# A gather ring that also borrows the buffers of rows needed later, and products spread evenly over a tile

## The reference, cut to what matters

```
xn  = layernorm(x)
xp  = xn @ W                                   # 4 heads of 256
e   = leaky_relu(a_src[src] + a_dst[dst])      # per edge and head, also a loop per node
alpha = softmax of e over the edges of a destination
x1  = x + relu(segment_sum(xp[src] * alpha, dst) + bias)
out = x1 + quantize(layernorm(x1)) @ quantize(weight).T + ffn_bias
```

## Time and profile before

| | |
|---|---|
| median of 3 runs | 1280.57 us |
| the profiled execution's own time | 1283.93 us |
| its span | 1282.0 us |
| busy: PE, PEld, DVE, ACT, POOL | 79%, 45%, 75%, 51%, 55% of the span |
| gathers (queue 0) | 211.80 MB |
| mean granted clock of TensorE | 0.898 of full |
| last stage | about 482 to 1282 us |

### The profile page before, as it was taken

One profiled execution on the slowest core, in us unless ns is written; L12 is line 12 of the kernel. 1 busy time (PEld: TensorE's weight loads), 2 busy tenths in 40 slices (PEclk: granted clock), 3 DMA queues, 4 the chain that ended last, 5 costly groups with the idle time before them and its releaser, 6 DMA issues.

```text
span 1282.0 us, 32738 instructions
## 1 busy us (share of the span) xinstructions
PE 1009.4 (79%) x12460; PEld 574.0 (45%) x12485; DVE 961.6 (75%) x2213; ACT 654.6 (51%) x887; POOL 711.3 (55%) x668
## 2 busy tenths in 40 slices
PE   8799488899999985556767777888888778877764
PEld 6678244455445532333433444444444444444332
DVE  6998899988986346666676778888878888778650
ACT  4566488788446534233342554544554544455541
POOL 1000367666214735765667777777777777777100
PEclk9899699999999996557887999898999999989888
DMA  7686358655347538888999999999999999999310
GB/s 276 204 302 242 80 177 305 208 175 167 99 148 222 168 119 294 294 271 268 328 317 331 329 375 379 363 359 363 381 366 358 354 356 358 366 342 354 136 40 23
DMA packets 126624, 339.75 MB, mean 265 GB/s; under 512 B 33135, under 2 KB 46719, under 8 KB 126218
## 3 DMA queue, kind: packets, MB, share of 16 engines
q0 software_dynamic: 75104, 211.80, 46.6%
q1 hardware_dynamic: 48010, 125.00, 28.0%
q10 hardware_dynamic: 3360, 0.91, 0.4%
HBM read 331.32 MB, written 56.04 MB: 302 GB/s over the span
## 4 chain that ended last, share of the span: by engine, by line
DMA 21%; PE 17%; issue 9%; POOL 6%; DVE 5%; ACT 3%; DVEq 1%; POOLq 0%; ACTq 0%
DMA xg<-d_xp,tables 14%; PE fmm_ps L2115 9%; PE sum_ps L2087 6%; DMA acc<-d_xp,tables 4%; POOL xg L1824 4%; POOL acc L1824 2%; DMA acc<-d_xp,first_idx 2%; PE ftr_ps L2099 2%; DVE acc L1864 1%; ACT own_row L2011 1%; DMA xg<-d_xp,first_idx 1%; PE fmm_ps L2112 0%; DVE acc L1931 0%; DVE fscale L1922 0%; ACT q L2028 0%
## 5 line engine op out<-in xcount | busy, mean ns | idle before, releaser
L1824 POOL DMA_INDIRECT xg<-d_xp,tables x292 | 312.9, 1072 | 120.8 <-issue 70.0
L2011 ACT ACTIVATE own_row<-acc,ratio 32x256 f32<-32x256 f32 x392 | 197.9, 505 | 244.1 <-DVE acc L1889 231.7
L2115 PE MATMUL fmm_ps<-wdT,xqT 128*128 128x512 f16 x1200 | 312.8, 407 | 0.0
L1864 DVE TENSOR_TENSOR acc<-sum_ps,acc 128x258 f32 x488 | 205.9, 422 | 115.9 <-PE sum_ps L2090 104.8
L1605 PE MATMUL xp_ps<-acc 128*128 128x512 f16 x1152 | 262.9, 381 | 7.4 <-DVE acc L1163 4.7
L2087 PE MATMUL sum_ps<-xg,tables 128*32 128x256 f16 x3564 | 169.8, 308 | 118.8 <-DMA xg<-d_xp,tables 43.6
L1824 POOL DMA_INDIRECT acc<-d_xp,tables x186 | 199.4, 1072 | 62.4 <-issue 42.4
L2115 PEld LDWEIGHTS fmm_ps<-wdT,xqT 128*128 128x128 f16 x1200 | 115.9, 104 | 146.1 <-issue 40.5
L1605 PEld LDWEIGHTS xp_ps<-acc 128*128 128x128 f16 x1152 | 109.1, 98 | 128.5 <-DVE acc L1163 4.5
L2087 PEld LDWEIGHTS sum_ps<-xg,tables 128*32 128x32 f16 x3564 | 75.4, 102 | 203.4 <-issue 94.2
L2087 PE MATMUL sum_ps<-acc,tables 128*32 128x256 f16 x2292 | 96.6, 281 | 49.6 <-DMA acc<-d_xp,tables 34.4
(11 more groups left out here) (353 smaller groups left out, 1632.7 us busy)
## 6 DMA issues: line engine op xcount, KB each, us to landing
d_xnT<-acc SPq DMA_DIRECT2D x25, 512.0 KB, 3.7
own_row<-d_own SPq DMA_DIRECT2D x25, 512.0 KB
wdT<-in_x_dram SPq DMA_DIRECT2D x24, 512.0 KB, 5.0
acc<-d_xnT SPq DMA_DIRECT2D x24, 512.0 KB, 4.9
d_xp<-acc SPq DMA_DIRECT2D x24, 512.0 KB
d_own<-acc SPq DMA_DIRECT2D x96, 128.0 KB
tables<-d_lo SPq DMA_DIRECT2D x33, 320.0 KB, 4.9
xr<-in_x_dram SPq DMA_DIRECT2D x16, 512.0 KB, 7.2
```

The lines of the kernel that those rows point to most:

```text
L1824: nc.gpsimd.indirect_dma_start(out=xg[j].rearrange("p a n -> p (a n)"), out_offset=None, in_=d_xp, in_offset=bass.IndirectOffsetOnAxis(ap= ...
L1864: nc.vector.tensor_tensor(out=to, in0=sum_ps[k % SB][:, 0:AW], in1=to, op=ALU.add).then_inc(added, 1)
L2011: last = nc.scalar.activation(own_row[r % 2][q * WIN:(q + 1) * WIN, h * C:(h + 1) * C], sums[rows, r * TILE_WINS + q, 0:C], ACT.Relu, scal ...
L2115: last = nc.tensor.matmul(mm_ps[:, cols], xqT[:, a, c, :], wdT[:, c, b, cols], start=False, stop=(c == KC - 1 and a == 1), skip_group_chec ...
```

## The change

- `ring_of_slots`: four more buffers take gathers from slot 0 on, each until a given slot: the buffer of normalised rows `xn` (until 28), `xr[0]` (20), `xr[1]` (38) and `own_row[0]` (9). Slots 0 to 8 so have nine buffers, then fewer, and from 41 to 53 five as before. The five spare places join at slot READY[j] + 14 (54, 75, 95, 115, 136), before at READY[j] + 40 (80, 101, 121, 141, 162), and their first gather waits for `moved` of the tile (the end of `move(j, 1)`) where it waited for the transposition.
- Normalised rows have one buffer of their own, `xn`, so the spare places hold them no more; `norm(r)` also waits for the transposition of tile r-1. Small scratch tiles lie in the end of `tables`, which was unused.
- The first loads of `own_row[0]`, `xr[0]` and `xr[1]` wait for the last gather slot in them (8, 15 and 35), the load of `own_row[1]` goes ahead of those of x, and the third load of x waits for `moved` of tile 0.
- `CHUNK` is 5 where it was 7: 10 bundles (9 of 5, one of 3) behind every second slot, 20 of 20.3 slots.

```
+EARLY = {"xn": 28, "xr0": 20, "xr1": 38, "own0": 9}
+FIRST_SPARE = RING + len(EARLY)
...
-    free_from = [(0, j) for j in range(RING)] + [(READY[j] + TURN_AT + 8, RING + n) for n, j in enumerate(SPARE_TILES)]
+    free = [(0, SLOTS_ALL, j) for j in range(RING)] + [(0, until, RING + n) for n, until in enumerate(EARLY.values())]
+    free += [(READY[j] + 14, SLOTS_ALL, FIRST_SPARE + n) for n, j in enumerate(SPARE_TILES)]
...
-    CHUNK = 7
+    CHUNK = 5
...
+        xn = sb("xn", [P, D])[:, :]
+        xg += [a.bitcast(F16).rearrange("p (a n) -> p a n", a=2)
+               for a in [xn, xr[0], xr[1], own_row[0][:, :]] + [of_tile(j) for j in SPARE_TILES]]
...
             def load_own(r):
+                if r == 0:
+                    sp.wait_ge(slot_done, EARLY_LAST["own0"] + 1)
...
             def load_x(r):
+                if r < 2:
+                    sp.wait_ge(slot_done, EARLY_LAST[f"xr{r}"] + 1)
                 if r == 2:
-                    sp.wait_ge(tr_done, 1)
+                    sp.wait_ge(moved, mixes(0))
...
-                elif j >= RING:
-                    pool.wait_ge(tr_done, SPARE_TILES[j - RING] + 1)
+                elif j >= FIRST_SPARE:
+                    pool.wait_ge(moved, mixes(SPARE_TILES[j - FIRST_SPARE]))
...
             def norm(r):
+                if r == 0:
+                    act.wait_ge(slot_done, EARLY_LAST["xn"] + 1)
+                else:
+                    act.wait_ge(tr_done, r)
```

More of the change, by code:

```diff
@@ L54 @@
 SPARE_TILES = range(1, 6)
+EARLY = {"xn": 28, "xr0": 20, "xr1": 38, "own0": 9}
+FIRST_SPARE = RING + len(EARLY)
 def ring_of_slots():
-    free_from = [(0, j) for j in range(RING)] + [(READY[j] + TURN_AT + 8, RING + n) for n, j in enumerate(SPARE_TILES)]
+    free = [(0, SLOTS_ALL, j) for j in range(RING)] + [(0, until, RING + n) for n, until in enumerate(EARLY.values())]
+    free += [(READY[j] + 14, SLOTS_ALL, FIRST_SPARE + n) for n, j in enumerate(SPARE_TILES)]
     used, places = {}, []
     for k in range(SLOTS_ALL):
-        j = min((used.get(b, -1), b) for since, b in free_from if since <= k)[1]
+        j = min((used.get(b, -1), b) for since, until, b in free if since <= k < until)[1]
         places.append((j, used.get(j)))
         used[j] = k
-    return places
-PLACES = ring_of_slots()
+    return places, {name: used[RING + n] for n, name in enumerate(EARLY)}
+PLACES, EARLY_LAST = ring_of_slots()
 FRESH = [k for k, (_, before) in enumerate(PLACES) if before is None]
@@ L1700, in gather_and_finish @@
         bias_parts = sb("fbias_parts", [P, D], BF16)
-        bias_ones = sb("fbias_ones", [P, P], BF16)
-        self_hn = sb("self_hn", [P, TILES, TILE_WINS])
+        bias_ones = tables[:, 6160 - P // 2:6160].bitcast(BF16)
+        left = tables[:, 10 * KT + (HB * HOTS * WIN + WB * PAIR * V * WIN) // 2:6160]
+        self_hn = left[:, 0:TILES * TILE_WINS].rearrange("p (t q) -> p t q", q=TILE_WINS)
+        scale, inv = left[:, 100:100 + QB], left[:, 132:132 + QB]
         self_r = sb("self_r", [P, TILE_WINS])
@@ L1708, in gather_and_finish @@
         in_scale = sb("fin_scale", [P, 1])
[L1709 to L1716, removed]
+        stats = left[:, 164:176].rearrange("p (a b) -> p a b", b=6)
+        mv = [left[:, 176 + 2 * j:178 + 2 * j] for j in range(2)]
+        std = [left[:, 180 + j:181 + j] for j in range(2)]
+        rstd = [left[:, 182 + j:183 + j] for j in range(2)]
+        shift = [left[:, 184 + j:185 + j] for j in range(2)]
+        newton = left[:, 186:187]
         sum_ps = [ps(f"sum_ps{j}", [P, 512]) for j in range(SB)]
@@ L1721, in gather_and_finish @@
         cleared = sem("cleared")
-        arrived = [sem(f"arrived{j}") for j in range(len(xg))]
+        arrived = [sem(f"arrived{j}") for j in range(RING + len(SPARE_TILES))]
         hot_ready = sem("hot_ready")
@@ L1751, in gather_and_finish @@
         landed = []
+        signal = lambda j: j if j < FIRST_SPARE else RING + j - FIRST_SPARE
         for j, _ in PLACES:
[L1753 to L1754 removed]
+            arrivals[signal(j)] = arrivals.get(signal(j), 0) + 1
+            landed.append(16 * arrivals[signal(j)])
         CLEAR = ((KC * D, 33 * D // 2), (33 * D // 2, WINS * AW))
@@ L1921, in scales @@
                 dve.wait_ge(xn_ready, r + 1)
-                own.link(nc.vector.tensor_reduce(out=scale[:, :], in_=blocks(xn(r)), axis=AX.X, op=ALU.max, apply_absolute_value=True))
+                own.link(nc.vector.tensor_reduce(out=scale[:, :], in_=blocks(xn), axis=AX.X, op=ALU.max, apply_absolute_value=True))
                 own.link(nc.vector.tensor_scalar(scale[:, :], scale[:, :], 1.0 / QMAX, 1e-30, ALU.mult, ALU.max))
@@ L1926, in to_grid @@
             def to_grid(r):
-                nc.vector.tensor_tensor(out=blocks(xn(r)), in0=blocks(xn(r)), in1=spread(inv[:, :]), op=ALU.mult).then_inc(y_ready, 1)
+                nc.vector.tensor_tensor(out=blocks(xn), in0=blocks(xn), in1=spread(inv[:, :]), op=ALU.mult).then_inc(y_ready, 1)
             def rescale(r):
                 dve.wait_ge(grid_ready, r + 1)
-                nc.vector.tensor_tensor(out=blocks(xn(r)), in0=blocks(q8[:, :]), in1=spread(scale[:, :]), op=ALU.mult).then_inc(xq_ready, 1)
+                nc.vector.tensor_tensor(out=blocks(xn), in0=blocks(q8[:, :]), in1=spread(scale[:, :]), op=ALU.mult).then_inc(xq_ready, 1)
             def low(r):
@@ L2019, in norm @@
             def norm(r):
+                if r == 0:
+                    act.wait_ge(slot_done, EARLY_LAST["xn"] + 1)
+                else:
+                    act.wait_ge(tr_done, r)
                 act.wait_ge(rstd_ready, r + 1)
-                nc.scalar.activation(xn(r), xr[r % 3], ACT.Identity, bias=shift[r % 2][:, :],
+                nc.scalar.activation(xn, xr[r % 3], ACT.Identity, bias=shift[r % 2][:, :],
                                      scale=rstd[r % 2][:, :]).then_inc(xn_ready, 1)
@@ L2027, in grid @@
                     act.wait_ge(xq_ready, r)
-                nc.scalar.activation(q8[:, :], xn(r), ACT.Identity, bias=tie[:, :], scale=GRID_DOWN, saturate=False).then_inc(grid_ready, 1)
+                nc.scalar.activation(q8[:, :], xn, ACT.Identity, bias=tie[:, :], scale=GRID_DOWN, saturate=False).then_inc(grid_ready, 1)
             def open_product(r):
@@ L2098, in turned @@
                 for c in range(KC):
-                    last = nc.tensor.transpose(tr_ps[:, c * P:(c + 1) * P], xn(r)[:, c * P:(c + 1) * P], ident[:, :])
+                    last = nc.tensor.transpose(tr_ps[:, c * P:(c + 1) * P], xn[:, c * P:(c + 1) * P], ident[:, :])
                 last.then_inc(tr_done, 1)
```

8 lines of the change are left out of this document (3 added, 5 removed).

## The result

The changed kernel takes 1312.14 us (median of 4 runs, 1310.23 to 1315.29) against 1281.53 us of the kernel before on the same chip: ratio 1.0241, interval 1.0212 to 1.0269. It is slower by 31 us where 10 us of gain were forecast. The profiled execution has a span of 1313.3 us against 1282.0.

The account below looks back on a forecast made before the run. Issue and transfers were taken to bound the later gathers, too few buffers those before 708.1 us. Terms -9 -9 +0 +8.4 gave -9.6 us: 1274.3 from the profiled 1283.93, as a median 1271, range 1255 to 1290.

Parts of the forecast that it names:

- sum of -9.6 us: Whole kernel: all terms added, -9 -9 +0 +8.4, against the profiled execution's 1283.93 us.
- later gathers: Last stage, 352 gathers from slot 136 on: bundles of five cost 0 us, bounds -5 and +28.
- second part: Last stage, slots 54 to 136: 127 us instead of 136.3, 9 saved, bounds 0 and 20.
- three signs set for being wrong: Slot 136 before 680 or after 700 us; later gathers over 1.39 us each; end not longer than now.
- The rival for slower: `low` blocks VectorE in each tile, 10 to 28 us over 17.3 tiles: 1281 to 1299, chance 0.20.
- the early part: Last stage before slot 136: earlier and additional buffers save 18 us together.
- the rival for faster: Before slot 136, moves end sooner and gathers land faster: gain 27, less 8.4, giving 1262 us; chance 0.22.
- The first part: Last stage, slots 0 to 53: nine buffers at first save 9 us, bounds 4 and 13.
- The tail: Behind the last gather: later `norm(22)` and 18 products behind the transposition cost 8.4 us, bounds 4 and 11.
- At nothing: Four more `first_idx` operations and late loads of x: no cost; if unhidden, 0.6 us and some 7 us once.

Follow-up runs that it names:

- experiment 2: Kernel before with bundles of five instead of seven, its ring and readiness untouched: ratio 1.0242.
- experiment 6: Changed kernel with bundles of six instead of five and the spare places free from 22 slots behind the writer instead of 14: 1267.47 us, ratio 0.9882.
- experiment 8: Changed kernel with four ring buffers instead of five and a second `xqT`, still bundles of five and 14 slots: 1285.85 us, ratio 1.0035.
- experiment 11: Changed kernel with the spare places free from 22 slots behind the writer instead of 14, nothing else: 1292.15 us, ratio 1.0088.
- second trace of the kernel before: Kernel before, unchanged, run again for its trace beside later runs: ratio 0.9998.
- experiment 1: Changed kernel with bundles of seven instead of five, its ring and buffers kept: ratio 1.0019.
- first set: First four follow-up runs, in which every execution took some 16% longer; the kernel before had a median of 1489.8 us there.

## Why the prediction was wrong

Against the sum of -9.6 us stand +31.4 measured in the two profiled executions. Of the 41.0 us between them 18.5 lie in the later gathers, 14.4 in the second part, 5.8 in the first and 2.3 at the end. Of the three signs set for being wrong two came: slot 136 went at 710.2, after 700, and the later gathers took 1.43 us each, over 1.39. The third did not: the end is longer, as forecast.

**The later gathers, "I take 0 for the 352 later gathers": failed, +18.5 us.** The place was named (`low` two to four slots ahead of the last bundle, with adds and weights queued behind it), and its price was wrong. I counted 1.02 + 1.21 + 0.42 + 0.42 = 3.1 us where it is four slots and 1.5 less where it is two, some 35 us over the 17 tiles, against 48.1 us in which TensorE waited for rows. The cover was there and was used: the waits for rows fell by 41.7 us. But the waits of the chain rose by 63.2: `opened` by 28.5, the transposition by 20.9, the tables by 13.8.

What was missing, by tile: in the twelve tiles with two slots, what ScalarE has queued behind `high` (`deviation`, `final`, `open_product`, 2.4 us of operations), which made nine of them stand 3.0 to 3.6 us; in three of the five with four slots, `spreads`, 898.78 to 900.48 in the timeline above, which stands at the same place of VectorE's order behind `low` and is 1.7 us, so that these stand 4.9 us; and in eleven tiles a wait of up to 2.7 us for `rescale`, ahead of the bundles, which I had not counted at all. The lower clock behind the longest stands (0.33 us per twelve products of a slot, 0.66 per three products of a bundle) adds little to the 18.5: TensorE's busy time rose by 1.9 us (the trace holds 87 fewer of its instructions than before, so a few us more are possible), and the granted clock of the stretch, 0.93, lies between the two of the kernel before.

Experiments 2, 6, 8 and 11 show that this hand-over is the loss behind slot 136: bundles of five alone bring it, six don't, a second `xqT` takes it away with bundles of five left as they are, and the readiness of the buffers leaves it untouched.

**The rival for slower** had this mechanism (chance 0.20), with a bound from the other side: the wait costs only what exceeds VectorE's 5.1 idle us per tile, 10 to 28 us. 18.5 lies within, but by luck: VectorE stood at `low` for 39.2 us, 2.3 per tile and less than half of those 5.1, and the time was lost all the same. In the sum the rival still counted the early part at -18, so 1281 to 1299 ended below 1312.

**The second part, "9 saved": failed in this ring, +5.4 us.** Against the second trace of the kernel before it is +11.3. The wait for `moved` was foreseen, with its period of 30.3 us from one to the next. Measured are 35.0, 34.6, 33.9 and 38.2. I let the move end with slot READY + 10, though the trace before had READY + 11 and + 13. Tile 4: the gather of slot 95 at 638.13, that of slot 111 at 659.00, slot 111 done at 668.07. The 29.9 us are close to the 30.3 only because two errors cancel: it was 20.9 us for 16 gathers where I counted 23.8 for 17.3, and 9.1 from the gather to the end of its slot where I took 6.5. The move ends at 670.98 and the next such gather leaves at 672.05, 4 us later. Part of this is VectorE, held at `low` and late to add and mix (slot 100 was done at 651.89 and added at 656.25, behind a `high` at 648.18 that had stood 10.8 us for products). It is not the main part: in experiments 1 and 8, where VectorE hardly waits at `low`, the five gathers still wait 19.4 and 16.0 us for `moved`, against 29.9 here. The readiness of 14 slots was itself too early. With 22 and five ring buffers the 9 us are there, and more: 121.2, 122.4 and 122.8 us against 130.4 and 136.3. (The 5.3 us of the earlier trace rows, which the rival for faster took as the time of a gather, hold 0.83 us of the slot itself: its first product starts at 502.51, 4.5 us after the issue.)

**The first part, -9: not reached in this ring.** The forecast had the gather of slot 54 at 562.8; it left at 568.52, after 3.34 us of the first wait for `moved`. From the first gather to it are 86.8 us, against 88.9 and 88.1 in the two traces of before. Up to the gather of slot 53, ahead of that wait, it is 82.5 us against 87.6 and 85.2, and with the same ring up to there experiments 11 and 6 have 78.1 and 79.2: a gain of 3 to 9.5 us. Most of it comes from nine gathers without a wait.

**The tail, +8.4: within its bounds, 10.7 measured.** The 18 products behind the transposition brought 5.1 us where 5.9 were set, and the late `norm(22)` 5.5 where 2.5 were set. Experiment 8 shows on what this depends: these products cost only because `high` waits for them. With two `xqT` the same 18 stand in the same place and the tail is 91.2 us.

**At nothing** (four more `first_idx`, the later loads of x): the stage began 1.1 us earlier, the first use of x moved from 541.80 to 534.04 without a wait (533 forecast), and neither VectorE nor ScalarE has a wait for a transfer in its list for the last stage. Nothing contradicts these terms.

## What to carry to other kernels

When work is spread over the whole period of a pipeline, every single-buffered value between two periods loses its slack: list for each what stands between its last reader and its next first reader, on every engine, with all that is queued at the same place. Count behind each step what the engine has queued there as well: here ScalarE's `final` and `open_product` stood behind a late `high` in nine tiles of 17. And a buffer that comes free by a long chain is better claimed late: on an engine that issues in order, one wait for it holds every later transfer too (20.5 us here for eight slots).

## What the runs showed of the hardware

- TensorE's granted clock over the later gathers was 0.94 and 0.92 in two executions of the kernel before, 0.93 in the change and 0.98 with two `xqT`. In the change it was 0.50 from 901.47 on, behind an idle time of 4.98 us, with 0.83 us per twelve products of a slot instead of 0.50; from 786.00 to 790.00, across the end of an idle time of 3.12 us, it was 1.00.
- Eight slots' delay of the five later buffers raised the transfers' rate between slots 54 and 136 from 298 to 335 GB/s (the change and experiment 11).
- In the first set transfers ran at 295 GB/s in the later gathers (experiment 1) where they run at 361 in the kernel before, with VectorE's adds and ScalarE's moves as long as ever (0.42 and 0.51 us each); bundles of five were 2.4% slower than the kernel before in either condition (experiment 2 and the change).
